# A language-model tower on one core: where TensorE's queue puts its small products within a turn

## The reference, cut to what matters

```python
# attention with a decaying state, per row of tokens
x_t    = 0.97 * x_state + relu(v @ Dx.T);  x_t /= sum(abs(x_t))
a_star = rho @ x_t
y_t    = relu(ln(a_star) @ Dy.T) * relu(x_t)
v_star = ln(y_t @ E.T)
rho    = 0.97 * rho + ln(v)[:, None] * x_t[None, :]
...
# eight experts, two of them weighted per token
logits = xn @ Wr + br                    # top 2, softmax -> w
y      = sum_e w[e] * (gelu(xn @ W1[e] + b1[e]) @ W2[e] + b2[e])
```

## Time and profile before

| | |
|---|---|
| median of 3 runs | 684.34 us (684.22 to 685.77) |
| profiled execution | 684.15 us, of it span 682.4 us |
| granted TensorE clock, mean of the span | 0.992 |
| TensorE busy | 631.3 us (93%) |
| VectorE busy | 530.5 us (78%) |
| ScalarE busy | 448.7 us (66%) |
| GpSimd busy | 343.1 us (50%) |

### The profile page before, as it was taken

The page is one execution under the profiler, slowest core; times in us unless marked ns, Lnnn a source line. Parts: engine busy times, 40 slices in busy tenths (PEclk is TensorE's granted clock), DMA queues, the critical chain, the costliest instruction groups (busy, mean ns, idle before and its releaser), DMA issues.

```text
span 682.4 us, 19223 instructions
## 1 busy us (share of the span) xinstructions
PE 631.3 (93%) x5077; PEld 432.5 (63%) x5077; DVE 530.5 (78%) x1953; ACT 448.7 (66%) x1385; POOL 343.1 (50%) x440
## 2 busy tenths in 40 slices
PE   2582997999999999999999999999999999999998
PEld 0471774456667667666667777776776666667635
DVE  4998888976777788888888778887777888887664
ACT  6990998014566667777666677667776667776673
POOL 2000000944356666665566666666556666655553
PEclk9999999889999999999999999999999999999999
DMA  6200000001444444444454455544444444444464
GB/s 205 114 0 0 2 0 1 7 33 62 95 95 103 102 101 101 101 102 101 104 117 110 114 113 111 116 121 101 101 101 101 101 101 101 102 101 103 87 118 94
DMA packets 61471, 60.42 MB, mean 89 GB/s; under 512 B 21972, under 2 KB 56900, under 8 KB 60932
## 3 DMA queue, kind: packets, MB, share of 16 engines
q1 hardware_dynamic: 59012, 59.35, 36.6%
q10 hardware_dynamic: 2240, 0.73, 0.4%
q0 software_dynamic: 192, 0.01, 0.0%
HBM read 55.19 MB, written 4.89 MB: 88 GB/s over the span
## 4 chain that ended last, share of the span: by engine, by line
PE 84%; DVE 9%; ACT 2%; issue 2%; DMA 1%; SPq 0%; POOL 0%; ACTq 0%; DVEq 0%; POOLq 0%
PE bank L1571 15%; PE bank L1441 13%; PE bank L1559 8%; PE bank L1560 7%; PE bank L1502 5%; PE bank L1522 4%; PE bank L1463 4%; PE bank L1476 3%; PE bank L1452 2%; PE bank L1480 2%; PE bank L1336 2%; PE bank L1298 2%; PE bank L1430 2%; PE bank L1347 2%; PE bank L1327 2%
## 5 line engine op out<-in xcount | busy, mean ns | idle before, releaser
L644 ACT ACTIVATE skill_rows<-bank,b1T,w_scale 128x512 f32<-128x512 f32 x256 | 196.6, 777 | 19.9 <-PE bank L1560 14.0
L478 POOL TENSOR_TENSOR feat_parts<-skill_rows 128x512 f32<-128x512 f32 x62 | 78.9, 1273 | 90.3 <-DVE feat_parts L1043 85.8
L1571 PE MATMUL bank<-skill_rows,w_sb 128*64 128x256 f32 x928 | 116.4, 382 | 0.0
L1441 PE MATMUL bank<-feat_parts 128*128 128x256 f32 (+1 forms) x512 | 102.2, 333 | 1.4 <-DVE feat_parts L1043 0.9
L1571 PEld LDWEIGHTS bank<-skill_rows,w_sb 128*64 128x64 f32 x928 | 63.1, 137 | 37.4 <-issue 11.0
L1441 PEld LDWEIGHTS bank<-feat_parts 128*128 128x128 f32 x512 | 79.6, 191 | 7.3 <-DVE feat_parts L1043 1.6
L1043 DVE TENSOR_TENSOR_SCAN feat_parts<-same,feat_parts 128x512 f32<-128x512 f32 x62 | 72.2, 1205 | 0.0
L1049 DVE TENSOR_TENSOR feat_parts<-bank,mask_sb 128x128 f32<-128x128 f32 x128 | 36.3, 284 | 38.6 <-PE bank L1441 37.7
L668 ACT ACTIVATE bank<-bank 128x64 f32<-128x64 f32 x128 | 26.6, 220 | 50.9 <-PE bank L1531 50.9
L1136 DVE SCALAR_TENSOR_TENSOR skill_rows<-bank,b2T,skill_rows 128x256 f32<-128x256 f32 x120 | 49.7, 475 | 3.6 <-PE bank L1571 2.5
L1065 DVE SCALAR_TENSOR_TENSOR feat_parts<-bank,feat_parts 128x256 f32<-128x256 f32 x128 | 45.0, 412 | 7.7 <-PE bank L1502 7.7
(11 more groups left out here) (278 smaller groups left out, 1526.1 us busy)
## 6 DMA issues: line engine op xcount, KB each, us to landing
skill_rows<-w_d SPq DMA_DIRECT2D x32, 512.0 KB, 6.6
same<-factor_d SPq DMA_DIRECT2D x31, 512.0 KB, 5.5
feat_parts<-w_d SPq DMA_DIRECT2D x30, 512.0 KB, 6.1
skill_rows<-skill_row_d SPq DMA_DIRECT2D x4, 1024.0 KB, 7.9
out<-o_sb SPq DMA_DIRECT2D x28, 128.0 KB, 5.1
feat_parts<-w_d SPq DMA_DIRECT2D x4, 256.0 KB, 4.8
w_sb<-in_L_ffn_W ACTq DMA_DIRECT2D x2, 256.0 KB
w_d<-wT SPq DMA_DIRECT2D x32, 16.0 KB, 1.4
```

The source lines that it names most:

```text
L478: pool.tensor_tensor(half[:, n, :], tm[:, 2 * n, :], tm[:, 2 * n + 1, :], ALU.add).then_inc(po_half, 1)
L644: act.activation(hid[:, e, :], banks[e % len(banks)][:, :], ACT.Gelu, bias=b1T[:, e:e + 1], scale=w1_scale[:, e:e + 1]).then_inc(ac_gelu, 1)
L1441: last = pe.matmul(n_bank[sc % 2][:, 0:SPAN[sc]], xs[:, k, sc * P:(sc + 1) * P], xs[:, k, sc * P:sc * P + SPAN[sc]], start=(k == 0), stop= ...
L1571: last = pe.matmul(z_bank[q % 2][n * D:(n + 1) * D, at:at + S // 2], w2_sb[:, e, :], hid[:, e, n * (S // 2):(n + 1) * (S // 2)], start=Tru ...
```

## The change

`state_of` and `attn_var` now issue one product per call, and `hidden` is divided into `hidden_high` and `hidden_low`. The waits stay in front of the first product, the semaphore is still raised by the last. The four state products go each behind one half of the third and the fourth first layer, the two variance products behind the high half and the low half of the sixth, and the logits go ahead of the second first layer instead of behind it.

```diff
-            def state_of(b):
-                pe.wait_ge(po_ub, b + 1)
...
+            def state_of(b, k, c):
+                if k + c == 0:
+                    pe.wait_ge(po_ub, b + 1)
+                    pe.wait_ge(ac_rows, b + 1)
+                    wait(pe, dv_tm, NP * (b - 3) if not isinstance(b, int) or b >= 4 else 0)
+                last = pe.matmul(zB[:, k * D:(k + 1) * D], x_rows[:, c, k * P:(k + 1) * P], ub[:, c, :],
+                                 start=(c == 0), stop=(c == 1))
+                if k + c == 2:
+                    last.then_inc(pe_state, 1)
...
+            def hidden_low(b, e, side):
+                pe.matmul(h_bank[e % 2][:, :], w1k[:, 1, e, :], xT[side][:], start=False, stop=True).then_inc(pe_hid, 1)
...
+                if rt:
+                    logits(t, side)
                 if mlp:
                     hidden(k, 1, 1 - side)
-                if rt:
-                    logits(t, side)
                 if att:
                     scores(i, 2)
                     scores(i, 3)
+                for n in range(NK):
+                    if mlp:
+                        hidden_high(k, 2 + n, 1 - side)
+                    if att:
+                        state_of(i, n, 0)
+                    if mlp:
+                        hidden_low(k, 2 + n, 1 - side)
+                    if att:
+                        state_of(i, n, 1)
                 if mlp:
-                    hidden(k, 2, 1 - side)
-                if att:
-                    state_of(i)
-                if mlp:
-                    hidden(k, 3, 1 - side)
                     expert_out(k, 0, i)
...
                 if mlp:
-                    hidden(k, 5, 1 - side)
+                    hidden_high(k, 5, 1 - side)
                 if att:
-                    attn_var(i)
+                    attn_var(i, 0)
+                if mlp:
+                    hidden_low(k, 5, 1 - side)
+                if att:
+                    attn_var(i, 1)
                 if ahead:
                     update(i + 1, 0)
```

More of the change, by code:

```diff
@@ L1505, in y_core, with attn_var @@
                             last.then_inc(pe_y, 1)
[L1507 to L1515, removed]
+            def attn_var(b, n):
+                if n == 0:
+                    pe.wait_ge(ac_sq, b + 1)
+                    if isinstance(b, int) and b == 0:
+                        pe.wait_ge(ones_set, 4)
+                last = pe.matmul(az[:, C * D + 2 * n:C * D + 2 * n + 2], a_sq[:, n * P:(n + 1) * P], ones_d[:, n, :],
+                                 start=True, stop=True)
+                if n == 1:
+                    last.then_inc(pe_var, 1)
             def z_out(b):
@@ L1552, in logits, with hidden_high @@
                 last.then_inc(pe_lg, 1)
-            def hidden(b, e, side):
+            def hidden_high(b, e, side):
                 if isinstance(b, int) and b + e == 0:
@@ L1559, in hidden @@
                 pe.matmul(h_bank[e % 2][:, :], w1k[:, 0, e, :], xT[side][:], start=True, stop=False)
+            def hidden_low(b, e, side):
                 pe.matmul(h_bank[e % 2][:, :], w1k[:, 1, e, :], xT[side][:], start=False, stop=True).then_inc(pe_hid, 1)
+            def hidden(b, e, side):
+                hidden_high(b, e, side)
+                hidden_low(b, e, side)
             def expert_out(b, q, turn_now=None):
```

## The result

The changed kernel takes 679.75 us in the median of five runs (678.37 to 681.76), against 684.34 before (684.08 to 685.77, five runs). The ratio is 0.9931, with a 95% interval of 0.9918 to 0.9944. Measured again later, beside two other kernels, it took 678.78 (678.27 to 679.14) against 684.30, a ratio of 0.9916 (0.9902 to 0.9929). Its profiled execution took 678.37 us with a span of 676.6; against the 684.15 of the one before it is 5.8 us shorter.

What follows compares the result with a forecast made beforehand. TensorE's own queue was taken to fill the 16.13 us turn. Of 0.335 us saved, 0.168 + 0.083 = 0.25 would remain; over 29 turns 7.2 us, 684.15 - 7.2 = 676.9 us, range 674.2 to 680.5.

Steps and rivals of the forecast that it cites:

- State 0.168: Four state products between first-layer halves: each hides one of two weight loads, 0.672 us instead of 0.840, saving 0.168 per turn.
- logits 0.083: Logits ahead of the second first layer: a half layer hides the next score product's float32 load, saving 0.083 us per turn.
- variance 0.084: Variance products around the sixth layer's low half: 0.28 us instead of 0.36, 0.084 off TensorE, but lost waiting for the gelu.
- (c): Rival, 5%: loads not hidden or each return to a half costs 0.056 us; only the logits' gain stands, 683 to 684.
- (d): Rival, 4%: leaving a half with open accumulation drains the array, 0.09 us per change, 8.6 us slower, 692.7 us.
- The sentence of the Trainium skill: By this rule no load here would be hidden, gain zero, time 684; the forecast followed the trace instead, 0.25 us a turn.
- The fifth gelu: The seventh first layer waits for it; its path stays 1.33 us while TensorE's work falls to 1.25, losing 0.084 us.
- the update behind it can start at 417.94: Update behind VectorE's second gate product, where TensorE wants 417.89; its 0.216 us ends at 418.16, ahead of the seventh layer at 418.19.
- The end of the gate: VectorE's second gate product was to end about 0.09 us earlier, at 417.87 instead of 417.96.
- the prediction's own sign of its path: Seventh layer should start later behind the update than 0.216 us, by 0.03 to 0.1, its load right behind the fifth gelu.
- Rival (b): 18%: ScalarE's later state copy holds the path, fourth gelu not before 412.94; gain 0.17 us per turn, 679.2 us.
- It did move, to 0.17 behind the state copy, as forecast: Fourth gelu on ScalarE was to start 0.16 us behind the state copy, at 412.85 instead of 412.94.

Runs made afterwards that it cites:

- the kernel with both chains shortened: Changed kernel with ScalarE's routing tanh moved ahead of the state copy and the gelus' two waits exchanged: turn 15.800 us, 675.98 us, ratio 0.9867.
- the tanh first: Changed kernel with ScalarE's routing tanh ahead of the state copy instead of behind the squares: turn 15.880 us, 677.51 us, ratio 0.9897.
- both edits on ScalarE and TensorE's order of before: Kernel before, with the routing tanh ahead of the state copy and the gelus' two waits exchanged: turn 16.127 us, 684.38 us, ratio 0.9998.

## Why the prediction was right, and where it was off

**The prices of the products** were right to a hundredth, each by TensorE's own starts and all together. State 0.168, logits 0.083 and variance 0.084 sum to 0.335, and the kernel with both chains shortened shows 0.333. The first of a product's two loads is hidden behind the half of an open accumulation, and the second shows as before (0.168 us for a product), so rivals (c) and (d) fell. The sentence of the Trainium skill weighed in the prediction ("TensorE: Matmul & The Clock Gate", section "The mechanism"), that a load overlaps matmuls in flight only where the row groups differ, does not hold in these turns. The same section also lets loads into a background weight buffer run ahead; no run here can tell whether these are such loads.

**The fifth gelu** was judged rightly too. The variance products alone gave nothing, in either kernel, and the seventh layer starts 0.05 us behind the fifth gelu where it waits for it (402.26 and 402.31 above). With the tanh first the turn is the one forecast, 15.880 for 15.88.

**The step that failed** is one sentence of the prediction on VectorE: "the update behind it can start at 417.94". That lets 0.07 us pass between the end of the second gate product and the update, and no row stands behind the 0.07. In the changed kernel the end is at 415.11 and the weight load at 415.25, 0.14 us. The end of the gate was forecast rightly, 11.16 us behind the first score product by both accounts (417.87 - 406.71, 415.11 - 403.95). With 0.14 the update comes so late that its 0.216 us end behind the fifth gelu, and the seventh layer starts 0.05 to 0.06 us later than the gelu alone would let it. 29 x 0.05 = 1.5 us, which is about the whole difference between 676.9 and the profiled 678.37. So the prediction's own sign of its path, a seventh layer that starts later behind the update than 0.216 us, is absent in the changed kernel, where the layer follows the update at once; it appears only with the tanh first. In the kernel before the second gate ends at 417.96 and the update's load stands at 418.11, also 0.14 to 0.15, but there TensorE's queue explains that time by itself (with both edits on ScalarE and TensorE's order of before, the gate ends 0.24 us sooner and the turn is only 0.006 shorter), and I did not ask whether the wait ended any sooner. The one wait of TensorE that the prediction had read, that of the seventh layer behind the gelu, took 0.05 us in the loop (418.38 to 418.43), and there no register instruction follows the wait. The earlier trace rows held a warning that such times differ: in the last turn the same wait took 0.14 us (644.16 to 644.30).

So the mechanism at that place was a mixture of mine and of rival (b). Rival (b) had the state copy's chain holding the turn, but through a fourth gelu that did not move. It did move, to 0.17 behind the state copy, as forecast. The chain bound all the same, by its tail. The gain of 0.194 us a turn lies nearer to rival (b)'s 0.17 than to the forecast's 0.25, and the first median, 679.75, nearer to its 679.2 than to 676.9. That the result lies in the range owes something to luck: the range took in rival (b), at 18%, and not a longer wait behind the gate.

**The rest**, from 678.37 to the median of 679.75, is spread. The later five runs lie at 678.78. Long adds (0.3 us each, three in one traced execution) and a preparation of varying length (the first state copy comes between 145.2 and 147.8 us in the traces of all kernels here) are both seen; their shares in those runs stay open.

## What to carry to other kernels

A float32 product with many weight columns and few streamed ones is paid by its weight load. It is two passes with a load each. Put the product behind a long pass and the first load is free, also in the middle of an open accumulation; the second is not. Of the 0.335 us a turn that this order can give, 0.194 came with nothing else touched. When one engine fills its turn exactly, work out every wait that it meets after the saving, in hundredths of a microsecond and with the latency of that very wait, because the nearest two bounds may lie 0.05 us apart and both have to go. Then look at what the other engines do ahead of the thing waited for: moving one tanh of 0.2 us and exchanging two waits brought the turn from 15.939 to 15.800 here, some 4 us over 29 turns, and nothing without the change on TensorE.

## What the runs showed of the hardware

A second wait whose value sits in a register costs a register instruction behind the first: the gelu starts 0.11 us behind its layer, and 0.03 when the wait that is always met comes first. In the loop TensorE's load for the seventh layer starts 0.05 us behind the end of the gelu that it waits for, and its load for the update 0.14 us behind the gate that it waits for, with a register instruction of 0.05 us between; no run takes that instruction away. A small VectorE add with both inputs in SBUF lasts 1.31 in place of 0.19 us where a GpSimd add of 1.27 us started 6 or 7 ns before it, and 0.19 where the lead was 5 ns or less; with one input in PSUM it keeps 0.19 us at a lead of 13 ns.
